# A gated cross-attention and mixture-of-experts block on one Trainium2 core: who places the value strips, and when three small pieces of routing work run

## The chip, the core and the metric

One core of a Trainium2 chip, one launch. Its engines run side by side, each in the order of its own instruction queue, and meet only through semaphores: TensorE (PE), VectorE (DVE), ScalarE (ACT), GpSimd (POOL) and SyncE (SP, which here only issues DMAs). The metric is the device time of one launch in microseconds (us). The kernel before takes 487.54 us, the median of 3 runs (487.33 to 488.08).

## The reference

Two residual steps on x of shape (8, 256, 256), all in float32:

```
q = layernorm(x) @ wq + bq;  k = ctx @ wk + bk;  v = ctx @ wv + bv        # 16 heads of 16, 77 context rows
score = q k^T / 4 * mask;  score = where(score == 0, -1e9, score)
x = x + tanh(g_xattn) * ((softmax(score) v) @ wo + bo)
n = layernorm(x);  probs = softmax(n @ router_w + router_b)               # 4 experts, the best 2 of each token
x = x + tanh(g_ffn) * sum over the 2 experts of gate * ((silu(n @ w1) * (n @ w3)) @ w2)
```

## The kernel before

**Two halves.** Attention runs batch by batch (b = 0 to 7); from about 158 us on the experts run over "slots" of 256 grouped tokens, 16 full ones and 3 short ones, with each float32 product split into three fp32r products. Everything is unrolled by hand: each engine's function is a list of calls whose order is the order of its queue.

**Attention of one batch.** `turn_x(b)` (PE, L1540) transposes the normalized x that ACT's `norm(b)` (L831) has written; ACT's `xT_copy(b)` takes it from the PSUM bank `ps_misc`; `project_q(b)` (PE, L1547) makes the queries in the same bank, and `q_copy(b)` (ACT, L849 and L850) takes them to `qT`. `scores(b, g)` (PE, L1561) makes the scores of eight heads (g = 0 or 1). For each of the four strips s of a batch, DVE's `mask_scores` (L1308), `sink_zeros` (L1314) and `find_lowest` (L1319) prepare the softmax, POOL's `lower(b, s)` (L1149) subtracts the minimum, PE's `turn_p` (L1573, L1581) transposes, ACT's `probT_exp` (L862, L867) takes the exponential into SBUF, and PE's `attend` (L1593) multiplies with the values. ACT's `weighed_copy` (L874) brings the result back, DVE's `invert_sums` (L1326) inverts the sums, `context(b, g)` (L307, on POOL; for the last batch on DVE) divides, `turn_ctx` (PE, L1607) and `project_o` (PE, L1615) follow, and DVE's `residual` (L1294) adds.

**The values.** `values(i)` (PE, L1715) projects the values of two batches into one of four PSUM banks (`ps_vals`, the fourth is `ps_misc`), ACT's `vals_copy` (L945) takes them to `vals`. `place_values` (L738) then copies them with DMAs into the block matrix `vblock`: 12 strips (`STRIPS`), each 1 to 77 rows of 544 bytes, for batches 0 to 3 (i = 0), and 12 more for 4 to 7 (i = 1). Before the change SP issues 8 strips of i = 0 and all of i = 1, and ACT issues the last 4 of i = 0. SP issues the loads of the expert weights and the fill of `grouped` behind them.

**Routing.** Batches go in pairs (group k). After a pair, DVE's `variance2`, POOL's `deviation2(k)` (L331, L333, L335), ACT's `norm2` (L347) and PE's `turn2` (L359) and `route_product` (L374) make the logits; DVE's `logit` (L384), `compare`, `order_of`, `choose` (L412, L414) and `lag` pick the experts; `rank` (PE) and `places` (POOL) find each token's row, and POOL's `scatter` (L514) sends the rows to `grouped` in DRAM by indirect DMA. DVE's `hand_out(i)`, `hand_out_begin`, `hand_out_owner` and `hand_out_rest` (L524 to L568) turn the counts into slots: 20 small instructions for i = 0, 1, 2 each, counted by the semaphore `handed`. SP's load of slot 0's tokens (L782) waits for the 20th.

**Where they stand.** Group 0's hand-out (i = 0) runs on DVE in b = 6 (`hand_out(0)` after strip 0, `hand_out_begin` and `hand_out_owner` after strip 1) and in b = 7 (`hand_out_rest` after strip 1). Group 1's routing (logit to lag) stands behind it in b = 6. In b = 7 POOL does gates, fill, `context(6, 0)`, `lower(7, 0)`, places, one scatter, `lower(7, 1)`, `deviation2(2)`, `context(6, 1)`, `lower(7, 2)`, `lower(7, 3)`, and then seven scatters; PE's `turn_ctx(6)` and, behind it, `attend(7, 1)` and `turn_p(7, 2)` wait in its queue for `context(6, 1)`.

Of the kernel before, what the change touches and what calls it, by code (L numbers as in the profile page):

```python
# [16 lines left out]
P = 128  # L17
# [21 lines left out]
BY_ACT = 4  # L39
# [61 lines left out]
def flamingo_block(nc, x, ctx_t, mask, rows, columns, wq, wk, wv, wo, rw, w1, w3, w2, small_in, tokens_in, pad_in, out, grouped):  # L101

    with ExitStack() as keep:
# [136 lines left out]
        ps_vals = [ps_probT, ps_route, ps_wide, ps_misc]  # L240
# [25 lines left out]
        kblock_done = sem("kblock_done")  # L266
        ld_vblock = [sem(f"ld_vblock{i}") for i in range(2)]
# [69 lines left out]
        def norm2(act, k, some):  # L337
            act.wait_ge(off2_done, k + 1)
            if k == 0:

                for landed in ld_vblock:
                    act.wait_ge(landed, 16 * len(STRIPS))
# [109 lines left out]
        def fill(pool, k):  # L452

            pool.wait_ge(rt_step, ROUTE * k + 16)
            if k == 0:

                for landed in ld_vblock:
                    pool.wait_ge(landed, 16 * len(STRIPS))
# [61 lines left out]
        def hand_out(dve, i):  # L520

            at = HAND * i
            dve.wait_ge(ranked, i + 1)
            dve.scalar_tensor_tensor(out=count[:], in0=base, scalar=1.0 - TILE, in1=first_row,  # L524
                                     op0=ALU.add, op1=ALU.subtract).then_inc(handed, 1)
            dve.wait_ge(handed, at + 1)
# [204 lines left out]
        def place_values(eng, i, some):  # L731
# [5 lines left out]
            for c, h, r0, r1 in some:  # L737
                eng.dma_start(vblock[r0 - c * P:r1 - c * P, c, h - HEAD0[c], mine], vals[r0 - h * SK:r1 - h * SK, h, mine]).then_inc(ld_vblock[i], 16)  # L738

        with nc.Block(no_gpsimd_drain=True) as block:  # L740
            @block.sync
            def _(sp):
# [22 lines left out]
                place_values(sp, 0, STRIPS[:-BY_ACT])  # L765
                place_values(sp, 1, STRIPS)
# [47 lines left out]
            def _(act):  # L814
# [32 lines left out]
                def q_copy(b):  # L847
                    act.wait_ge(q_done, b + 1)
                    act.activation(qT[:, 0, :], ps_misc[:, 0:SQ], ACT.Identity, bias=bqs[:, 0:1]).then_inc(q_copied, 1)  # L849
# [30 lines left out]
                def body(b, first=False, last=False):  # L880
# [3 lines left out]
                    if not last:  # L884
                        norm(b + 1)
# [3 lines left out]
                    if not last:  # L889
                        xT_copy(b + 1)  # L890
# [64 lines left out]
                q_copy(0)  # L955
                vals_copy(2)
                vals_copy(3)
                place_values(act, 0, STRIPS[-BY_ACT:])
# [159 lines left out]
            def _(pool):  # L1118
# [33 lines left out]
                def body(b, first=False, last=False):  # L1152
# [15 lines left out]
                    if b in BEGIN:  # L1168
# [3 lines left out]
                    if not first:  # L1172
                        context(pool, b - 1, 1)
                    lower(b, 2)
# [32 lines left out]
                keys(0, 1)  # L1207

# [59 lines left out]
            def _(dve):  # L1268
# [59 lines left out]
                def body(b):  # L1328
                    for s in range(NS):
# [22 lines left out]
                        if (b, s) == (B - 2, 0):  # L1352
                            hand_out(dve, 0)
                        if (b, s) == (B - 2, 1):
                            hand_out_begin(dve, 0)
                            hand_out_owner(dve, 0)
                        if (b, s) == (B - 1, 1):
# [31 lines left out]
                context(dve, B - 1, 0)  # L1389
                hand_out(dve, 1)  # L1390
# [510 lines left out]
```

## Time and profile before

| | |
|---|---|
| median of 3 runs | 487.54 us |
| the profiled execution's own time | 488.64 us |
| its span in the profile | 486.70 us |
| mean granted TensorE clock, share of full | 0.989 |
| busy PE, DVE, ACT, POOL | 460.7, 378.6, 307.0, 196.0 us |

The span is 1.94 us shorter than the time of the same execution; the rest lies around it. Times in the rows below count from the start of the span. A matmul that is queued counts as busy, so PE's 95% does not say that its array was full.

### The profile page before, as it was taken

What the parts mean: (1) busy time and instruction counts of PE and PEld (TensorE: products, weight loads), DVE (VectorE), ACT (ScalarE), POOL (GpSimd) and SP (SyncE); (2) the same over time, 40 slices, a digit from 0 to 9 for tenths busy, and PEclk for the clock granted to TensorE, in tenths of its full rate; (3) what the DMA queues carried; (4) which work ended last, traced back from release to release, by engine and by line L of the source; (5) the groups of instructions that cost most, each with busy time, mean ns of one, the idle gap of its engine ahead of it and who ended that gap; (6) DMA issues with size and microseconds to landing.
All of it is one profiled execution on the core that took longest, in us unless ns stands there. A gap on an engine that the chain in (4) does not pass through costs nothing.

```text
span 486.7 us, 11552 instructions
## 1 busy us (share of the span) xinstructions
PE 460.7 (95%) x3720; PEld 433.4 (89%) x3720; DVE 378.6 (78%) x876; ACT 307.0 (63%) x768; POOL 196.0 (40%) x204
## 2 busy tenths in 40 slices
PE   7899899989869999999999999999999999999995
PEld 5578797877767999899999999999999999999894
DVE  1577998978964888886888888888878878878772
ACT  2426555464435667686767767777767767776782
POOL 4428686597784045342146253113303303302312
PEclk9989999999979999999999999999999999999999
DMA  8619998842113104032023132122112102102112
GB/s 256 162 42 392 380 410 312 335 179 90 39 50 112 47 22 90 12 80 24 23 31 70 38 66 45 24 44 26 33 33 44 21 22 33 22 13 34 23 13 23
DMA packets 33968, 45.22 MB, mean 93 GB/s; under 512 B 10183, under 2 KB 30613, under 8 KB 33685
## 3 DMA queue, kind: packets, MB, share of 16 engines
q1 hardware_dynamic: 25999, 35.21, 21.6%
q0 software_dynamic: 6576, 8.92, 10.9%
q10 hardware_dynamic: 1344, 0.48, 0.5%
q8 instruction: 26, 0.43, 0.4%
q14 instruction: 23, 0.19, 0.1%
HBM read 32.91 MB, written 21.82 MB: 112 GB/s over the span
## 4 chain that ended last, share of the span: by engine, by line
PE 68%; DVE 16%; ACT 5%; issue 4%; POOL 3%; ACTq 1%; DMA 1%; DVEq 0%; SPq 0%; POOLq 0%
PE ps_rows L1764 22%; PE ps_wide L1784 7%; PE ps_probT L1764 7%; PE ps_misc L1784 7%; PE ps_wide L1593 5%; DVE w_lo L1404 3%; PE ps_misc L1615 2%; PE ps_misc L1547 2%; PE ps_rows L1813 2%; DVE w_lo L1400 2%; PE ps_probT L1573 2%; PE ps_wide L1824 1%; PE ps_rows L1561 1%; DVE score L1314 1%; DVE ps_rows L1409 1%
## 5 line engine op out<-in xcount | busy, mean ns | idle before, releaser
L1227 POOL DMA_INDIRECT out_x<-y_out,meta x35 | 64.0, 1830 | 190.9 <-ACT y_out L1026 185.8
L1404 DVE TENSOR_TENSOR w_lo<-w,w_hi 128x512 fp32r<-128x512 f32 x152 | 104.1, 685 | 13.4 <-issue 6.6
L1764 PE MATMUL ps_rows<-xt_hi,w_hi 128*128 128x256 f32 x384 | 110.6, 288 | 0.2 <-DVE xt_lo L1418 0.2
L1764 PE MATMUL ps_rows<-xt_hi,w_lo 128*128 128x256 f32 x384 | 108.6, 283 | 0.0
L1764 PE MATMUL ps_rows<-xt_lo,w_hi 128*128 128x256 f32 x384 | 108.6, 283 | 0.0
L975 ACT CAST w_hi<-w 128x512 fp32r x152 | 95.2, 627 | 4.2 <-issue 3.9
L1764 PEld LDWEIGHTS ps_rows<-xt_hi,w_hi 128*128 128x128 f32 x384 | 73.6, 192 | 0.4 <-DVE xt_lo L1418 0.4
L1764 PEld LDWEIGHTS ps_rows<-xt_lo,w_hi 128*128 128x128 f32 x384 | 73.6, 192 | 0.0
L1764 PEld LDWEIGHTS ps_rows<-xt_hi,w_lo 128*128 128x128 f32 x384 | 73.5, 192 | 0.0
L989 ACT ACTIVATE act_g<-ps_rows 128x256 f32<-128x256 f32 x96 | 37.3, 389 | 28.7 <-PE ps_rows L1764 24.0
L1004 ACT CAST hid_hi<-ps_rows 128x256 fp32r<-128x256 f32 x96 | 36.1, 376 | 27.1 <-DVE ps_rows L1409 26.3
L1413 DVE TENSOR_TENSOR hid_lo<-ps_rows,hid_hi 128x256 fp32r<-128x256 f32 x96 | 40.5, 422 | 15.6 <-ACT hid_hi L1004 15.6
L1149 POOL TENSOR_TENSOR score<-score,lowest 128x616 f32<-128x616 f32 x32 | 41.5, 1297 | 22.1 <-DVE lowest L1319 21.8
L1593 PEld LDWEIGHTS ps_wide<-vblock,probT 128*128 128x128 f32 (+1 forms) x320 | 39.7, 196 | 10.5 <-ACT probT L867 10.2
L1400 DVE TENSOR_TENSOR w_lo<-w2s,w_hi 128x512 fp32r<-128x512 f32 x64 | 44.0, 688 | 5.8 <-ACT w_hi L982 5.8
L1593 PE MATMUL ps_wide<-vblock,probT 128*128 128x102 f32 (+2 forms) x320 | 42.0, 278 | 6.0 <-ACT probT L867 5.9
L1409 DVE TENSOR_TENSOR ps_rows<-act_g,ps_rows 128x256 f32<-128x256 f32 x96 | 40.6, 423 | 7.3 <-ACT act_g L989 6.0
L982 ACT CAST w_hi<-w2s 128x512 fp32r x64 | 39.7, 620 | 0.0
L514 POOL DMA_INDIRECT grouped<-shared,place_at x32 | 33.9, 1061 | 9.8 <-issue 8.7
L1784 PE MATMUL ps_misc<-w_hi,hid_hi 128*128 128x256 f32 x128 | 37.0, 289 | 0.6 <-DVE hid_lo L1413 0.5
L1784 PE MATMUL ps_wide<-w_hi,hid_hi 128*128 128x256 f32 x128 | 36.6, 286 | 0.1
L1764 PE MATMUL ps_probT<-xt_hi,w_hi 128*128 128x256 f32 x128 | 36.2, 283 | 0.0
(241 smaller groups left out, 1160.9 us busy)
## 6 DMA issues: line engine op xcount, KB each, us to landing
grouped<-in_pad SPq DMA_DIRECT2D x1, 10296.0 KB
w<-in_L_ffn_w SPq DMA_DIRECT2D x8, 1024.0 KB, 12.2
w2s<-in_L_ffn_w SPq DMA_DIRECT2D x4, 1024.0 KB, 13.7
xg<-grouped SPq DMA_DIRECT2D x16, 256.0 KB, 2.7
out_x<-xall SPq DMA_DIRECT2D x8, 256.0 KB, 7.0
xall<-in_x SPq DMA_DIRECT2D x1, 1024.0 KB, 12.6
xall<-in_x SPq DMA_DIRECT2D x1, 768.0 KB, 7.9
ctxT<-in_ctx_t SPq DMA_DIRECT2D x2, 308.0 KB, 5.4
```

What stands on the lines that cost most here:

```text
L975: act.copy(w_hi[:, f % NB], unit_weights(e, f)).then_inc(w_hi_done, 1)
L982: act.copy(w2_hi[:, q % 2], pair_w2(e, q)).then_inc(w2_hi_done, 1)
L989: act.activation(act_g[:, f % 2, 0:n], ps_gu[f % NB][:, 0, 0:n], ACT.Silu).then_inc(silu_done, 1)
L1149: pool.tensor_tensor(score[:, s], score[:, s], lowest[:, s].unsqueeze(2).to_broadcast([P, HG, SK]), ALU.subtract).then_inc(lowered, 1)
L1227: pool.indirect_dma_start(out, bass.IndirectOffsetOnAxis(ap=meta[:, s % 2, t, E:E + 1].bitcast(U32), axis=0), y_out[:, s % 2, t, :], None, ...
L1400: dve.tensor_tensor(w2_lo[:, q % 2], pair_w2(e, q), w2_hi[:, q % 2].bitcast(F32), ALU.subtract).then_inc(w2_lo_done, 1)
L1404: dve.tensor_tensor(w_lo[:, f % NB], unit_weights(e, f), w_hi[:, f % NB].bitcast(F32), ALU.subtract).then_inc(w_lo_done, 1)
L1409: dve.tensor_tensor(ps_gu[f % NB][:, 1, 0:n], act_g[:, f % 2, 0:n], ps_gu[f % NB][:, 1, 0:n], ALU.mult).then_inc(hid_done, 1)
L1413: dve.tensor_tensor(hid_lo[:, f % NB, 0:n], ps_gu[f % NB][:, 1, 0:n], hid_hi[:, f % NB, 0:n].bitcast(F32), ALU.subtract).then_inc(hid_lo_d ...
L1593: mm = pe.matmul(ps_av[:, :, HEAD0[c]:HEAD0[c] + HEADS[c], :], probT[0:ROWS[c], s % 2, c, :], vblock[0:ROWS[c], c, 0:HEADS[c], b].rearrang ...
L1764: mm = pe.matmul(ps_gu[f % NB][:, m, 0:n], lhs, rhs[:, a, c, 0:n], start=(k == 0), stop=(k % (3 * DC) == 3 * DC - 1), skip_group_check=True)
L1784: mm = pe.matmul(ps_y[a][:, t], lhs, w, start=(f == 0 and t == 0 and i == 0), stop=(f == FC - 1 and i == 2), skip_group_check=True)
```

## The change

It does five things.

1. The last 4 strips of i = 0 are issued by POOL in place of ACT, after `keys(0, 1)` and before its first `lower`. They count on a semaphore of their own, `ld_vblock_end`, which `attend(0, 0)`, `norm2` and `fill` wait for as well.
2. ACT does `norm(1)` right after `q_copy(0)`, and `xT_copy(1)` after the copies of `values(1)`. PE does `turn_x(1)` ahead of `values(2)` and `project_q(1)` ahead of `values(3)`.
3. `values(3)` goes to the bank `ps_probT` (after the copies of `values(0)`), so `turn_x(1)` no longer waits for all value copies. `q_copy(b)` waits, for b above 0, for the scores of the batch before.
4. In b = 7, POOL does `context(6, 1)` before `deviation2(2)`.
5. The first instruction of a hand-out is a function of its own, `hand_out_count`. For i = 0 it alone stays in b = 6; the other four instructions of `hand_out(0)` go to b = 7 after strip 1, and begin, owner and rest to b = 7 after strip 3.

```diff
-        ps_vals = [ps_probT, ps_route, ps_wide, ps_misc]
+        ps_vals = [ps_probT, ps_route, ps_wide, ps_probT]
...
-        def hand_out(dve, i):
-
-            at = HAND * i
+        def hand_out_count(dve, i):
             dve.wait_ge(ranked, i + 1)
             dve.scalar_tensor_tensor(out=count[:], in0=base, ...).then_inc(handed, 1)
+
+        def hand_out(dve, i):
+            at = HAND * i
             dve.wait_ge(handed, at + 1)
...
-                place_values(sp, 0, STRIPS[:-BY_ACT])
-                place_values(sp, 1, STRIPS)
+                place_values(sp, 0, STRIPS[:-BY_POOL], ld_vblock[0])
+                place_values(sp, 1, STRIPS, ld_vblock[1])
...
                 def q_copy(b):
                     act.wait_ge(q_done, b + 1)
+                    if b:
+                        act.wait_ge(scores_done, RG * DC * b)
...
                 vals_copy(0)
                 vals_copy(1)
                 q_copy(0)
+                norm(1)
                 vals_copy(2)
                 vals_copy(3)
-                place_values(act, 0, STRIPS[-BY_ACT:])
+                xT_copy(1)
                 for b in range(B // 2, B):
                     vals_copy(b)
...
-                    if b in BEGIN:
+                    if b in BEGIN and not last:
                         deviation2(pool, BEGIN[b])
...
                     if not first:
                         context(pool, b - 1, 1)
+                    if last:
+                        deviation2(pool, BEGIN[b])
                     lower(b, 2)
...
                 keys(0, 1)
+                place_values(pool, 0, STRIPS[-BY_POOL:], ld_vblock_end)
                 body(0, first=True)
...
                         if (b, s) == (B - 2, 0):
-                            hand_out(dve, 0)
-                        if (b, s) == (B - 2, 1):
+                            hand_out_count(dve, 0)
+                        if (b, s) == (B - 1, 1):
+                            hand_out(dve, 0)
+                        if (b, s) == (B - 1, 3):
                             hand_out_begin(dve, 0)
                             hand_out_owner(dve, 0)
-                        if (b, s) == (B - 1, 1):
                             hand_out_rest(dve, 0)
...
                 scores(0, 0, True)
+                turn_x(1)
                 values(2)
-                pe.wait_ge(q_copied, 2)
+                project_q(1)
+                pe.wait_ge(vals_copied, 2)
                 values(3)
-                turn_x(1)
                 scores(0, 1, True)
-                project_q(1)
                 body(0, first=True)
```

## Rows read from the trace of the kernel before

**Rows 1.** Page, part 4: engines on the chain that ended last.

```profile
PE 68%; DVE 16%; ACT 5%; issue 4%; POOL 3%; ACTq 1%; DMA 1%; DVEq 0%; SPq 0%; POOLq 0%
```

**Rows 2.** Timeline, 14 to 34 us: start, us, engine, line, work, count, idle before.

```profile
14.13 1.89 PE L1547 MATMUL ps_misc<-xnT,wqs 128*128 128x256 f32 x8
16.43 0.47 ACT L850 ACTIVATE qT<-ps_misc,column_in 128x256 f32<-128x256 f32 x1
17.68 0.81 PE L1561 MATMUL ps_rows<-kblock,qT 32*128 32x154 f32 x16
18.54 3.79 ACTq L738 DMA_DIRECT2D vblock<-shared  x4
26.57 2.91 PE L1547 MATMUL ps_misc<-xnT,wqs 128*128 128x256 f32 x8
26.79 1.51 DVE L1308 TENSOR_TENSOR score<-ps_rows,maskt 128x616 f32<-128x616 f32 x2 [3.51 <-PE ps_rows L1561]
29.32 0.60 PE L1573 MATMUL ps_probT<-small,score 128*128 128x128 f32 x4
30.77 1.33 PE L1593 MATMUL ps_wide<-vblock,probT 128*128 128x68 f32 x10 [0.75 <-ACT probT L867]
33.53 1.51 DVE L1308 TENSOR_TENSOR score<-ps_rows,maskt 128x616 f32<-128x616 f32 x2 [0.27 <-PE ps_rows L1561]
```

**Rows 3.** Windows: stretch, length, busy PE, PEld, DVE, ACT, POOL, PEclk, DMA, GB/s.

```profile
22.00:25.00 3.00, 0.51 (x5) 0.42 (x4) 1.25 (x2) 2.17 (x6) 3.00 (x3) 1.00 0.19 49
107.00:108.40 1.40, 0.90 (x7) 0.47 (x5) 0.84 (x2) 0.99 (x4) 1.22 (x1) 1.00 0.00 0
126.00:128.00 2.00, 0.54 (x5) 0.39 (x3) 1.93 (x6) 0.27 (x1) 1.92 (x3) 1.00 0.19 68
138.00:141.00 3.00, 0.77 (x5) 0.52 (x5) 2.97 (x5) 0.77 (x2) 2.83 (x5) 1.00 0.34 87
141.00:148.00 7.00, 6.52 (x26) 6.04 (x27) 2.50 (x13) 2.61 (x6) 5.99 (x6) 0.51 0.11 39
```

**Rows 4.** Groups by line, POOL's DMAs: busy us, mean ns, idle before.

```profile
L1227 POOL DMA_INDIRECT out_x<-y_out,meta x35 | 64.0, 1830 | 190.9 <-ACT y_out L1026 185.8 <-issue 5.1
L514 POOL DMA_INDIRECT grouped<-shared,place_at x32 | 33.9, 1061 | 9.8 <-issue 8.7 <-POOL place_at L504 1.1
```

**Rows 5.** Timeline of b = 6, 113 to 128 us.

```profile
113.56 0.19 DVE L527 TENSOR_TENSOR begun<-count,small 128x32 f32<-128x32 f32 x1
115.88 0.16 DVE L538 TENSOR_REDUCE last_slot<-fresh_until 128x4 f32<-128x16 f32 x1
117.36 1.94 PE L374 MATMUL ps_route<-rws,ctxT 128*128 128x64 f32 x16
118.12 1.50 DVE L1308 TENSOR_TENSOR score<-ps_rows,maskt 128x616 f32<-128x616 f32 x2
121.07 0.16 DVE L384 TENSOR_TENSOR logits<-ps_route,row_in 128x16 f32<-128x16 f32 x1
127.70 0.39 PE L475 MATMUL ps_route<-places_base,one_row 1*128 1x20 f32 x2 [1.46 <-DVE chosen_b L414]
```

**Rows 6.** Timeline: deviation2(0) in b = 3, then b = 7, 137 to 146 us.

```profile
69.95 1.02 POOL L331 TENSOR_TENSOR rstd<-vareps,half 128x4 f32<-128x4 f32 x1
137.08 1.22 POOL L1149 TENSOR_TENSOR score<-score,lowest 128x616 f32<-128x616 f32 x1
138.26 1.62 POOL L331 TENSOR_TENSOR rstd<-vareps,half 128x4 f32<-128x4 f32 x1
138.90 0.24 DVE L1326 RECIPROCAL rden<-weighed 128x16 f32<-128x16 f32 x1
140.81 0.61 POOL L307 TENSOR_TENSOR ctxn<-weighed,rden 128x256 f32<-128x256 f32 x1
141.48 1.11 PE L1607 MATMUL ps_misc<-small,ctxn 128*128 128x128 f32 x4 [2.35 <-POOL ctxn L307]
144.42 1.06 PE L1573 MATMUL ps_probT<-small,score 128*128 128x128 f32 x4
```

More of the change, by code:

```diff
@@ L38 @@
 STRIPS = [(c, h, max(c * P, h * SK), min(c * P + ROWS[c], (h + 1) * SK)) for c in range(NC) for h in range(HEAD0[c], HEAD0[c] + HEADS[c])]
-BY_ACT = 4
+BY_POOL = 4
 NS = 2 * QT
@@ L266, in flamingo_block @@
         kblock_done = sem("kblock_done")
+        ld_vblock_end = sem("ld_vblock_end")
         ld_vblock = [sem(f"ld_vblock{i}") for i in range(2)]
@@ L339, in norm2 @@
             if k == 0:
-                for landed in ld_vblock:
-                    act.wait_ge(landed, 16 * len(STRIPS))
+                act.wait_ge(ld_vblock_end, 16 * BY_POOL)
+                act.wait_ge(ld_vblock[0], 16 * (len(STRIPS) - BY_POOL))
+                act.wait_ge(ld_vblock[1], 16 * len(STRIPS))
             if k > 1:
@@ L455, in fill @@
             if k == 0:
-                for landed in ld_vblock:
-                    pool.wait_ge(landed, 16 * len(STRIPS))
+                pool.wait_ge(ld_vblock_end, 16 * BY_POOL)
+                pool.wait_ge(ld_vblock[0], 16 * (len(STRIPS) - BY_POOL))
+                pool.wait_ge(ld_vblock[1], 16 * len(STRIPS))
             if k > 1:
@@ L729, in is_slot, with place_values @@
             return isinstance(s, int) and s == n
-        def place_values(eng, i, some):
+        def place_values(eng, i, some, landing):
             eng.wait_ge(vblock_cleared, 1)
@@ L737, in place_values @@
             for c, h, r0, r1 in some:
-                eng.dma_start(vblock[r0 - c * P:r1 - c * P, c, h - HEAD0[c], mine], vals[r0 - h * SK:r1 - h * SK, h, mine]).then_inc(ld_vblock[i], 16)
+                eng.dma_start(vblock[r0 - c * P:r1 - c * P, c, h - HEAD0[c], mine], vals[r0 - h * SK:r1 - h * SK, h, mine]).then_inc(landing, 16)
         with nc.Block(no_gpsimd_drain=True) as block:
@@ L883, in body @@
                         turned2_copy(act, BEGIN[b - 1], 2)
-                    if not last:
+                    if not last and not first:
                         norm(b + 1)
@@ L888, in body @@
                         probT_exp(b - 1, 3, False)
-                    if not last:
+                    if not last and not first:
                         xT_copy(b + 1)
@@ L1389, in _ @@
                 context(dve, B - 1, 0)
+                hand_out_count(dve, 1)
                 hand_out(dve, 1)
@@ L1485, in routing @@
                     if u == 8:
+                        hand_out_count(dve, 2)
                         hand_out(dve, 2)
@@ L1530, in turn_x @@
                         pe.wait_ge(q_copied, 2 * b)
-                    if b == 1:
-                        pe.wait_ge(vals_copied, B)
                     if b == 2:
@@ L1588, in attend @@
                         pe.wait_ge(weighed_done, n)
-                    if s == 0 and b % (B // 2) == 0:
-                        pe.wait_ge(ld_vblock[b // (B // 2)], 16 * len(STRIPS))
+                    if s == 0 and b == 0:
+                        pe.wait_ge(ld_vblock_end, 16 * BY_POOL)
+                        pe.wait_ge(ld_vblock[0], 16 * (len(STRIPS) - BY_POOL))
+                    if s == 0 and b == B // 2:
+                        pe.wait_ge(ld_vblock[1], 16 * len(STRIPS))
                     for c in range(NC):
```

## The prediction

> **What bounds the kernel now.** I read the page's chain shares first: PE carries 68% of the chain that ended last, DVE 16%, POOL 3%, ACT's DMA issue 1% [rows 1]. The expert half is PE on end and the change leaves it alone, so I followed the chain and the timeline only to 158 us, and looked at the three places that the diff touches. There the reader should see three stalls.
>
> First, in the prelude ACT issues four strips for 3.79 us from 18.54 on, and the copies of the later values, norm(1) and with it turn_x(1) stand behind them. PE is busy for 0.51 of the 3 us from 22 to 25 [rows 2, 3], its granted clock then falls to half, and project_q(1) takes 2.91 us where project_q(0) took 1.89. DVE has idled 3.51 us when mask_scores for strips 2 and 3 of batch 0 begins at 26.79 [rows 2]. From there to 33.53, the masks of batch 1, it has only 0.27 us idle [rows 2]: DVE is the bound of that stretch, PE's attend(0, 0) at 30.77 is not.
>
> Second, in b = 6 DVE is on the chain from 112.7 to 130, and the hand-out stands in its queue: four instructions from 113.56, nine from 115.88 to 118.12, before the masks of strips 2 and 3 [rows 5].
>
> Third, in b = 7 POOL is on the chain: lower(7, 1) at 137.08, deviation2(2) from 138.26, context(6, 1) only at 140.81, and PE, idle 2.35 us, starts turn_ctx(6) at 141.48 [rows 6]. The clock then is 0.51 over the 7 us from 141 to 148 [rows 3].
>
> **Prelude, edits 1 to 3.** q_copy(0) ends at 16.90 [rows 2]. norm(1) is 2 activations of some 0.55 us, so 18.05, in time for the copies of values(1), which are late by 0.2 us at most. scores(0, 0) starts at 17.68 and lasts 0.81 [rows 2]. Behind it PE runs without a wait: turn_x(1) at 18.5 (0.45 us of pipeline), values(2) 1.74 (eight matmuls as in project_q(0), whose 1.89 includes the last one's drain), project_q(1) 1.74, values(3) 1.74, so scores(0, 1) starts at 24.15 and the masks about 1 us behind it, at 25.15. That is 1.6 us before 26.79. The DVE block of 6.74 us to the masks of batch 1 [rows 2] keeps its length less the 0.27 of idle time: 31.65 for 33.53, a gain of 1.9. Behind it DVE had another 0.6 us of waiting for PE, which may go too, but POOL's bias additions come earlier and would then lie beside sink_zeros of batch 1; I leave it out and keep it as the lower end (gain 2.5). Batches 1 to 5 have no absolute time in them, so this moves along.
>
> POOL's four issues have no row. The nearest are its indirect DMAs, 1.06 us each plus 0.27 idle, 1.33 in all; the dearest are those of the experts at 1.83 [rows 4]. ACT's own issues of the same strips, 3.79 / 4 = 0.95 us, are the cheap end [rows 2]. Queued behind them are lower(0, 0), keys(1, 0) and lower(0, 1), for which PE's turn_p waits. With 1.33 each from 18.9, lower(0, 0) (1.22 [rows 6]) runs at 24.2 to 25.4 and attend(0, 0) follows 1.45 us after the transposes begin, as 29.32 to 30.77 [rows 2], so at 27. With 0.95 it is limited by PE instead, at 26.7. With 1.83, lower ends at 27.4 and attend is at 29. Before it was 30.77, and DVE's gain of 1.9 needs about 28.9. So the price hardly matters inside the rows' ends: 1.9 at the likely price, 1.7 at the dear end. SP's eighth strip is issued by 18.8 + 8 x 0.95 = 26.4 at ACT's pace, and some 2 us of flight would still be inside 28.9. SP begins its twelve other strips when the last values are copied (25.1), 0.2 to 0.6 later than now, and the weights and the fill of grouped move by that. Nobody waits: all DMA traffic is over by 107, 1.4 us before the first scatter at 108.4 [rows 3], and the fill stands ahead of the out writes in that traffic. The new wait of q_copy is for matmuls that PE has done before the transposes that q_copy's predecessor used, so nothing.
>
> One rule speaks against POOL. The Trainium skill, "SBUF — State Buffer", section "Who interferes with whom", says that GpSimd cannot write DMA descriptors while VectorE runs a two-port operation, and names copy, cast and tensor_scalar on SBUF. DVE runs none of these between 18.9 and 24, only the masks from PSUM, sink_zeros and find_lowest (no run shows a plain DMA of POOL beside them), so by the rule as written the sum stays; if each of these five operations blocked POOL too, some 4.7 us (estimate) would be added and the gain of the prelude would be about nil.
>
> **b = 6, edit 5.** Removed from DVE before the masks of strips 2 and 3: four instructions (113.56 to about 114.4, 0.86 us) and nine (115.88 to 118.12, 2.24), 3.1 us [rows 5]. Not all of it is gained, since logit(1) waits for route_product(1) on PE, 117.36 + 1.94 = 119.3. So logit comes at 119.35 and not 121.07: 1.7 us [rows 5]. rank waits 1.46 us for chosen_b and starts at 127.70 [rows 5]; chosen_b comes 1.7 earlier and PE reaches rank at 127.70 - 1.46 = 126.2, so 1.5 to 1.6 us. I take 1.6, as POOL's gates follow DVE and not PE. Ends: 1.0, if POOL's scatters and bias_add, which do not move by as much, hold lower(6, 3); 2.2, if compare's two instructions, which lie beside POOL work now, get shorter. The four instructions come back in b = 7 after strip 1, where 0.73 us of hand_out_rest goes: 0.13 us on DVE. The other fifteen take some 2.4 us (2.24 for the nine of rows 5 with one that was held up, 0.73 for the six of rest, less the hold-up) and run after strip 3, where DVE has nothing else until PE's attend(7, 1) is back. SP then loads slot 0's tokens around 142 in the new time, for a transpose that PE reaches 5 to 6 us later.
>
> **b = 7, edit 4.** With everything 1.6 earlier, lower(7, 1) ends at 136.7. context(6, 1) needs the sums of invert_sums(6, 1), at 138.90 + 0.24 now [rows 6] and at 137.3 to 137.6 then. It is done at 138.0 and turn_ctx(6) starts at 138.05 where it was 141.48. The next that is late is turn_p(7, 2) on PE, for lower(7, 2), which stands behind deviation2(2). That took 138.26 to 140.81, 2.55 us, with rstd 1.62; in b = 3, with DVE out of the way, rstd was 1.02 [rows 6] and the whole 1.6. In its new place rstd lies beside sink_zeros and the rest beside find_lowest: 2.2. So lower(7, 2) runs 140.2 to 141.4, and turn_p(7, 2) starts at 141.45 for 144.42: 3.0 us, of which 1.4 is edit 4's (ends 1.0 and 1.9 with 2.55 and 1.6).
>
> **The clock.** PE would now idle from the end of attend(7, 1), 139.7, to 141.45: 1.75 us. Its idle of 2.35 us here, and of 3 - 0.51 = 2.5 us in the prelude, was followed by the lower of its two levels (1.2 GHz); the 1.46 us before rank left it at the higher one (2.4 GHz) [rows 3, 5, 6]. 1.75 is nearer to that. If the clock holds, the work from turn_p(7, 2) to the end of project_o(6), 4.2 us now at half clock [rows 3, 6], takes 2.5: 1.6 us more. Norm2's copies and slot 0 hang on that chain.
>
> **Sum.** 1.9 + 1.6 + 1.4 + 1.6 = 6.5 us. I take 0.2 off for the small shifts left out (SP, the 0.13 us on DVE): 6.3. On the profiled execution that is 486.70 - 6.3 = 480.4 of span and 488.64 - 6.3 = 482.3 of time. The median of the runs lies 1.1 below that execution: 487.54 - 6.3 = 481.2.
>
> **Rivals.**
> - *The clock falls all the same in b = 7.* For it: 1.75 us is no row, and PE's idle time before it adds 0.6 us near 137.4. Against it: both falls had longer gaps. Then 1.6 is lost: 487.54 - 4.7 = 482.8.
> - *The prelude gives nothing*, because POOL's issues or the landing of its strips hold attend(0, 0) to 30 or later (the price per issue above 2.1 us), while b = 6 and 7 go as above: 487.54 - 4.4 = 483.1; with the clock's fall, 484.7.
> - *Slower: POOL's issues become the bound of the prelude.* Each costs p, and attend(0, 0) comes at 18.9 + 4p + 1.22 + 1.45. It passes 30.77 from p = 2.3, and the loss eats 3.0 us of b = 6 and 7 (clock fallen) from p = 3.05. At p = 3.6, 2.2 us are lost: 489.7. For it: nothing shows a plain DMA on this queue. Against it: 67 indirect ones at 1.06 and 1.83 [rows 4].
> - *Nothing moves*: the first two stalls turn out to be cover for another wait up to 158 us, as DVE's POOL partners in b = 1 and b = 6: 487.5.
>
> **How the numbers follow.** The forecast 0.46, the clock's fall 0.32, a prelude without gain 0.13, slower 0.05, nothing 0.04. The predicted time is the first's, 481.2. The low end takes the cheap ends together (2.5 + 2.0 + 1.7 + 1.6 = 7.8, less a bit): 479.9. The high end takes in the clock's fall and most of the third case: 484.6. A change of less than 0.2% (1.0 us) cannot be told from none. Faster 0.91, same 0.04, slower 0.05.
>
> **What would show it.** Masks of batch 0, strips 2 and 3, at 25.2 and of batch 1 at 31.7; the granted clock 1.00 from 25 to 28; POOL's four issues 1.0 to 1.4 us each and attend(0, 0) near 27. In b = 6, logit(1) right behind route_product(1), and rank straight behind attend(6, 1). In b = 7, turn_ctx(6) 0.6 us behind invert_sums(6, 1), PE idle under 2 us before turn_p(7, 2), and project_o(6) 1.9 us long. The first matmul of slot 0, now near 158.1, at 151.8. I am wrong if attend(0, 0) waits for a strip, if the clock reads 0.5 in b = 7, or if the gain at 54 us is gone again at 112.

## The result, and the profile after

The changed kernel takes 483.47 us, the median of 5 runs (482.7 to 485.29), against 487.54 us (487.1 to 488.08) for the kernel before in the same comparison: a ratio of 0.9925, with an interval of 0.9901 to 0.9949. The profiled execution took 483.3 us, its span 481.4 us, at a mean granted clock of 0.992. The forecast was 481.2 us, in a range of 479.9 to 484.6: the time lies in the range, 2.3 us above the forecast, and the signs that the first rival named (the clock falls all the same in b = 7, 482.8 us) are what the profile shows.

The start of q_copy(0) varies by up to 0.9 us between the executions profiled here (15.39 to 16.33), so places are also compared by their distance from it; it stands at 16.06 in the trace before and at 15.72 after.

| place | before | after | change behind q_copy(0) |
|---|---|---|---|
| masks of batch 1 | 33.53 | 31.19 | -2.00 |
| last mean_off of the prelude | 47.75 | 44.70 | -2.71 |
| rank of group 1 | 127.70 | 123.69 | -3.67 |
| turn_p(7, 2) | 144.42 | 139.22 | -4.86 |
| first matmul of slot 0 | 158.15 | 152.92 | -4.89 |

So by these two traces 2.71 us come up to the last mean_off (the prelude's place), 0.96 from there to rank (b = 6), 1.19 from b = 7 up to turn_p(7, 2), and 0.03 from there to slot 0, where 1.6 was forecast. They are differences between one execution of each kernel; how much of them a fall of the clock makes up is taken up with x4 and x7. The 0.34 us by which this execution started earlier belongs to no edit. The chain that ended last is made up much as before. Its engines, page of the changed kernel, part 4, the answer to [rows 1]: PE keeps its 68%, DVE has two points more and POOL one less.

```profile
PE 68%; DVE 18%; ACT 5%; issue 4%; POOL 2%; DMA 1%; ACTq 1%; DVEq 0%; SPq 0%; POOLq 0%
```

**Prelude.** Timeline of the changed kernel, 18 to 32 us (start, us, engine, line, work, count, idle before), the answer to [rows 2]:

```profile
18.80 2.41 POOL L743 DMA_DIRECT2D vblock<-shared  x4 [1.64 <-ACT shared L952]
...
20.30 1.89 PE L1559 MATMUL ps_misc<-xnT,wqs 128*128 128x256 f32 x8
...
24.80 1.51 DVE L1319 TENSOR_TENSOR score<-ps_rows,maskt 128x616 f32<-128x616 f32 x2 [1.85 <-PE ps_rows L1573]
...
26.16 1.33 PE L1608 MATMUL ps_wide<-vblock,probT 128*128 128x68 f32 x10 [0.75 <-ACT probT L874]
...
31.19 1.50 DVE L1319 TENSOR_TENSOR score<-ps_rows,maskt 128x616 f32<-128x616 f32 x2
```

The four issues take 0.60 us each on POOL, project_q(1) has its full clock (1.89 us for 2.91), and the masks wait 1.85 us for 3.51. attend(0, 0), forecast near 27, comes at 26.16, 4.6 us earlier than before, and what ends its wait is ACT's exponential, not a strip.

**b = 6.** Timeline of the changed kernel, 114 to 124 us, the answer to [rows 5]:

```profile
114.32 1.94 PE L376 MATMUL ps_route<-rws,ctxT 128*128 128x64 f32 x16
...
116.30 0.17 DVE L386 TENSOR_TENSOR logits<-ps_route,row_in 128x16 f32<-128x16 f32 x1 [0.57 <-PE ps_route L376]
...
116.51 3.17 DVE L394 TENSOR_TENSOR equal<-logits 128x64 f32<-128x64 f32 x1
...
116.58 0.63 POOL L308 TENSOR_TENSOR ctxn<-weighed,rden 128x256 f32<-128x256 f32 x1
...
117.15 1.22 POOL L1157 TENSOR_TENSOR score<-score,lowest 128x616 f32<-128x616 f32 x1
...
118.33 1.26 POOL L1151 TENSOR_TENSOR xall<-xall,row_in 128x512 f32<-128x512 f32 x1
...
119.61 0.21 DVE L395 TENSOR_TENSOR above<-logits 128x64 f32<-128x64 f32 x1
```

The logits come right behind the product, as forecast: 1.72 us earlier than before behind the last mean_off. Then `equal`, 64 elements, takes 3.17 us, where `above`, of the same shape, takes 0.21 right behind it. It ends at 119.68, 0.09 us after POOL's third operation in a row has ended. In the trace before the two took 2.56 us together, now 3.38: this step eats 0.8 of the 1.7 us.

**b = 7.** Timeline of the changed kernel, 134 to 153 us, the answer to [rows 6], and its windows around the clock's fall (columns as in [rows 3]), the answer to [rows 3]:

```profile
134.37 0.66 PE L1585 MATMUL ps_probT<-small,score 128*128 128x128 f32 x4 [0.70 <-POOL score L1157]
...
134.90 0.24 DVE L1337 RECIPROCAL rden<-weighed 128x16 f32<-128x16 f32 x1
...
135.22 0.62 POOL L308 TENSOR_TENSOR ctxn<-weighed,rden 128x256 f32<-128x256 f32 x1 [0.91 <-DVE rden L1337]
...
135.80 1.62 POOL L332 TENSOR_TENSOR rstd<-vareps,half 128x4 f32<-128x4 f32 x1
...
135.90 1.12 PE L1622 MATMUL ps_misc<-small,ctxn 128*128 128x128 f32 x4 [0.76 <-POOL ctxn L308]
...
139.22 1.12 PE L1585 MATMUL ps_probT<-small,score 128*128 128x128 f32 x4 [0.17 <-POOL score L1157]
...
140.34 3.02 PE L1630 MATMUL ps_misc<-wos,ctxnT 128*128 128x256 f32 x8
```

```profile
133.50:136.00 2.50, 1.03 (x8) 0.64 (x8) 2.50 (x5) 1.04 (x3) 1.59 (x3) 0.96 0.15 54
136.00:143.00 7.00, 6.83 (x27) 6.13 (x28) 6.52 (x25) 2.69 (x6) 6.21 (x7) 0.53 0.05 19
```

The order did what was wanted: turn_ctx(6) starts 0.76 us behind the end of invert_sums(6, 1), after a wait of 0.76 us where it was 2.35, and turn_p(7, 2) waits 0.17 us. But the clock goes to its lower level (1.2 GHz) at 135.8 and stays there until 142.6. That is before the wait that the prediction had weighed, and behind waits of 0.70 and 0.76 us; in the stretch from 133.5 to 136 PE was busy for 1.03 of 2.5 us. project_o(6) then takes 3.02 us.

### The profile page after: what moved, and what is told of

The parts are those of the page before. It is cut to its first block, busy times and chain, and to the rows that moved or that the text cites. A ratio compares the mean times of both kernels' runs of the same rounds, so it can differ in the third digit from the quotient of the medians.

```text
span 481.4 us, 11562 instructions
## 1 busy us (share of the span) xinstructions
PE 459.7 (95%) x3720; PEld 433.0 (90%) x3720; DVE 379.9 (79%) x876; ACT 306.8 (64%) x768; POOL 198.8 (41%) x208
## 4 chain that ended last, share of the span: by engine, by line
PE 68%; DVE 18%; ACT 5%; issue 4%; POOL 2%; DMA 1%; ACTq 1%; DVEq 0%; SPq 0%; POOLq 0%
PE ps_rows L1779 22%; PE ps_wide L1799 7%; PE ps_probT L1779 7%; PE ps_misc L1799 7%; PE ps_wide L1608 4%; DVE w_lo L1417 3%; PE ps_misc L1630 2%; PE ps_rows L1828 2%; DVE score L1325 2%; PE ps_misc L1559 2%; DVE w_lo L1413 2%; PE ps_probT L1585 2%; PE ps_wide L1839 1%; DVE score L1319 1%; PE ps_rows L1573 1%
```

## The experiments

The first four ran on one chip (kernel before there: 487.01 us), x5 to x8 on one (487.47), x9 to x11 on one (486.87), x12 alone (487.70). The theory going in: three separate gains, one for each place, and the clock's fall in b = 7 as a loss of its own that the order on POOL doesn't cure. The rival: one edit carries all.

**x1_changed**: the changed kernel again, beside its parts. No edit.

> The changed kernel itself, on the chip on which its parts run. Theory: 4.1 us less than before (the ratio measured so far, 0.9925), spread over some 2.5 us from run to run, because TensorE's granted clock falls for one stretch more in some executions than in others. Rival, that the spread is noise of other origin: then runs with the same mean granted clock differ as much as runs with different ones.

483.06 us, ratio 0.9911 (0.9883 to 0.9939). In its profile TensorE stays at the lower clock for 10.2 us in b = 7 and not for 6.8, and slot 0 comes 0.9 us later behind q_copy(0) (138.09 for 137.20): between these two executions a longer fall goes with about a microsecond.

**x2_prelude_only**: edits 1 to 3 alone.

```diff
-                    if b in BEGIN and not last:
+                    if b in BEGIN:
                         deviation2(pool, BEGIN[b])
...                  (context and hand-out as in the kernel before)
```

> Edits 1 to 3 alone (strips by GpSimd, the prelude's order, the bank), b = 6 and b = 7 as before. Theory, from the two traces: the prelude is worth 2.7 to 3.0 us, more than the 1.9 of the prediction, so 484.6 beside 487.5, and the first product of slot 0 at 155.1 to 155.4 where it was 158.15. Rival, the prediction's own sum: 1.9 us, 485.6. Second rival, the parts depend on each other and the prelude alone loses part of its gain again in b = 6: under 1.5 us.

485.22 us, ratio 0.9956 (0.9938 to 0.9974): -1.8 us. The last mean_off stands 28.98 behind the start of q_copy(0), as in the changed kernel.

**x3_context_first**: edit 4 alone, on the kernel before.

```diff
-                    if b in BEGIN:
+                    if b in BEGIN and not last:
                         deviation2(pool, BEGIN[b])
...
                         context(pool, b - 1, 1)
+                    if last:
+                        deviation2(pool, BEGIN[b])
```

> Edit 4 alone: in b = 7 GpSimd divides context(6, 1) before deviation2(2). Theory: turn_ctx(6) 1.6 us earlier (139.9 for 141.48), and turn_p(7, 2) 1.2 us earlier, for lower(7, 2) stands behind deviation2 in either order; 486.3 beside 487.5, with the clock falling as before. Rival, that the clock holds now that the wait is short: 1.6 us more, 484.7.

487.39 us, ratio 1.0002 (0.9972 to 1.0032): no gain in the time. Its profile has the step itself; timeline of this kernel, b = 7:

```profile
140.00 0.66 PE L1609 MATMUL ps_misc<-small,ctxn 128*128 128x128 f32 x4 [0.77 <-POOL ctxn L307]
...
143.33 1.11 PE L1575 MATMUL ps_probT<-small,score 128*128 128x128 f32 x4 [0.92 <-POOL score L1149]
...
144.45 3.49 PE L1617 MATMUL ps_misc<-wos,ctxnT 128*128 128x256 f32 x8
```

turn_p(7, 2) is 1.21 us earlier behind the last mean_off (95.46 for 96.67), the forecast's 1.4 nearly. But project_o(6) takes 3.49 us, nearly all of it at the lower clock (the fall lasts from 140.8 to 147.6), where it took 3.10, and slot 0 keeps 0.77 of the gain. That is within the interval of the time.

The 12 executions of this kernel lie between 483.62 us, at a mean granted clock of 0.999, and 490.25, at 0.982, and those of like clock agree within a microsecond (484.69 and 484.96 at 0.995, 489.06 and 489.14 at 0.985). This speaks for the theory put under x1, that the spread from run to run goes with the clock; the order on POOL does not keep the clock up.

**x4_handout_spread**: edit 5 alone.

```diff
                         if (b, s) == (B - 2, 0):
+                            hand_out_count(dve, 0)
+                        if (b, s) == (B - 1, 1):
                             hand_out(dve, 0)
-                        if (b, s) == (B - 2, 1):
+                        if (b, s) == (B - 1, 3):
                             hand_out_begin(dve, 0)
                             hand_out_owner(dve, 0)
-                        if (b, s) == (B - 1, 1):
                             hand_out_rest(dve, 0)
```

> Edit 5 alone: the hand-out of group 0 leaves b = 6. Theory, from the changed trace: 3.1 us of VectorE work goes but logit(1) gains 1.7 us only, and equal (the first of compare), which then meets GpSimd's context, lower and bias_add back to back, lasts some 3.2 us instead of 1.26, so that rank and all behind it gain 1.0 us: 486.5 beside 487.5. Rival, the prediction: 1.6 us, 485.9, with equal as long as before.

485.78 us, ratio 0.9969 (0.9949 to 0.9990): -1.2 us. Rank stands 78.96 behind the last mean_off, for 79.95 before: a gain of 0.99. Timeline of this kernel, b = 6: here `equal` is quick, and `above`, the next, waits in its place.

```profile
118.11 0.23 DVE L392 TENSOR_TENSOR equal<-logits 128x64 f32<-128x64 f32 x1
...
118.22 0.63 POOL L307 TENSOR_TENSOR ctxn<-weighed,rden 128x256 f32<-128x256 f32 x1
118.25 3.08 DVE L393 TENSOR_TENSOR above<-logits 128x64 f32<-128x64 f32 x1
```

Its prelude is the old one, and in this execution the clock did not fall at 25 us, as it did in the trace before: project_q(1) takes 1.99 us for 2.91 in [rows 2]. It fell later, at 37.2, for 3.4 us. Timeline of this kernel, and the window of that fall:

```profile
25.59 1.99 PE L1552 MATMUL ps_misc<-xnT,wqs 128*128 128x256 f32 x8
...
32.18 1.49 DVE L1310 TENSOR_TENSOR score<-ps_rows,maskt 128x616 f32<-128x616 f32 x2
...
39.60 1.50 DVE L1310 TENSOR_TENSOR score<-ps_rows,maskt 128x616 f32<-128x616 f32 x2 [0.65 <-PE ps_rows L1566]
```

```profile
37.20:40.60 3.40, 3.40 (x28) 2.74 (x26) 2.71 (x4) 1.08 (x4) 3.40 (x5) 0.51 1.03 422
```

So the comparison is clean only up to the masks of batch 1. They stand 16.45 us behind the start of q_copy(0) here, 17.47 in the trace before and 15.47 in the changed kernel: of the 2.00 us gained at that place, 0.98 is there with the clock up in both, and 1.02 goes with the fall at 25 us, which the profiled execution of the kernel before had and this one lacks. The last mean_off is 30.59 behind q_copy(0), 1.10 less than before and 1.61 more than in the changed kernel, but x4's own fall, with 0.65 us of waiting in it, lies ahead of that place.

The falls may well go with the old prelude's waits (PE waits 2.49 us for norm(1) in the trace before and here). All four traces that keep the old prelude have a fall ahead of the last mean_off, at 25.0, 24.8 (x3), 23.8 (x11) and 37.2 us (x4), and none of the eight with the new one has. Then the 1.02 us are the change's as well, but their size and place differ from one execution to the next, and no run separates the two.

From the last mean_off to slot 0 this kernel takes 108.15 us, the changed one 108.22 and the one before 110.40. Without edit 4, turn_p(7, 2) comes 16.72 us behind rank, with it 15.53, but the fall here (136.2 to 143.0) is over when project_o(6) starts, which takes 1.89 us. PE was busy for 4.91 of the 6.8 us of this fall, and for 6.53 of the 6.8 of the changed kernel's. What edit 4 gains at turn_p(7, 2) is thus not seen at slot 0 in this pair of traces.

**x7_pool_issue_only** and **x8_order_only** take the prelude apart: edit 1 alone, and edits 2 and 3 with ACT still issuing, after the second copy of values.

```diff
-                place_values(act, 0, STRIPS[-BY_ACT:])
...
                 keys(0, 1)
+                place_values(pool, 0, STRIPS[-BY_ACT:], ld_vblock_end)
```

```diff
                 vals_copy(3)
+                place_values(act, 0, STRIPS[-BY_POOL:], ld_vblock_end)
                 xT_copy(1)
...
-                place_values(pool, 0, STRIPS[-BY_POOL:], ld_vblock_end)
```

> The kernel before with edit 1 alone: GpSimd issues the four strips, order and banks of the prelude as before. Measured from the start of q_copy(0) to the last mean_off, which is 31.69 us before and 28.97 in the changed kernel, of which 1.1 us is a fall of the clock in the prelude that some executions have and others not. Theory: ScalarE is free of 3.8 us, but the copies of values(3) must still wait for that product, so norm(1) and turn_x(1) come only 0.5 us earlier: 31.1 with the fall, 30.0 without. Rival: the issues by ScalarE were the whole stall, and this alone brings the 2.7 us: 29.0.

> The changed kernel with the four strips issued by ScalarE again, at their old place, right after the copies of values(1): edits 2 and 3 without edit 1. Theory: xT_copy(1) now stands behind 3.8 us of issuing, project_q(1) waits for it and values(3) and scores(0, 1) behind that, so the masks of strips 2 and 3 come no earlier than before: 31.4 to 32 us from q_copy(0) to the last mean_off (31.69 before, 28.97 changed). Rival: the order alone brings most of it, since turn_x(1) is no longer behind the copies: 29.5.

x7 took 484.99 us and x8 486.27, one run each. Timelines of the two kernels, x7 first:

```profile
19.08 2.40 POOL L741 DMA_DIRECT2D vblock<-shared  x4 [1.61 <-ACT shared L948]
...
25.30 1.50 DVE L1311 TENSOR_TENSOR score<-ps_rows,maskt 128x616 f32<-128x616 f32 x2 [2.07 <-PE ps_rows L1564]
```

```profile
18.78 3.80 ACTq L743 DMA_DIRECT2D vblock<-shared  x4
...
22.62 0.59 ACT L850 COPY xnT<-ps_misc 128x512 f32<-128x512 f32 x1 [3.95 <-issue]
...
23.26 1.99 PE L1559 MATMUL ps_misc<-xnT,wqs 128*128 128x256 f32 x8 [2.23 <-ACT xnT L850]
...
27.86 1.50 DVE L1319 TENSOR_TENSOR score<-ps_rows,maskt 128x616 f32<-128x616 f32 x2 [4.34 <-PE ps_rows L1573]
```

Neither has a fall of the clock up to the last mean_off. The masks of batch 1 (31.69 in x7, 34.25 in x8) stand 15.68 behind the start of q_copy(0) in x7 and 17.95 in x8, against 16.45 in x4 and 15.47 in the changed kernel. At that place edit 1 alone gives 0.77 us; the new order alone costs 1.50, since project_q(1) then stands in PE's queue ahead of values(3) and scores(0, 1) and waits for a copy behind ACT's issues; together they give 0.98. The issue moved is what pays, and the new order adds 0.21 once ACT is free. These are places in one execution each; the two times, one run each, are too few for a verdict.

**x9_pool_issues_eight** asks how near the rival "POOL's issues become the bound" was.

```diff
-BY_POOL = 4
+BY_POOL = 8
```

> The changed kernel with BY_POOL = 8: GpSimd issues eight of the first set's strips, SyncE four. Theory: an issue on GpSimd costs 0.60 us here and nothing waits for GpSimd in the prelude until lower(0,0), so eight issues end 2.4 us later than four (at 23.6) and the path hardly feels it: lower(0,0) starts at 23.7 to 24.3 instead of near 22.5, the masks of batch 0's strips 2 and 3 stay at 24.8 (9.1 behind the start of q_copy(0)), the last mean_off stays 29.0 behind q_copy(0), within 0.3. Rival (the price that the slower rival of the prediction gave an issue, 3.05 us): lower(0,0) beyond 30 and mean_off 3 us or more later. Middle case: the issues stay cheap but turn_p(0,0) is then the last to wait, attend(0,0) comes up to 1.2 us later and mean_off with it by 0.5 to 1.2.

483.3 us, one run. Timeline of this kernel:

```profile
18.80 4.44 POOL L743 DMA_DIRECT2D vblock<-shared  x8 [1.61 <-ACT shared L952]
23.25 1.24 POOL L1157 TENSOR_TENSOR score<-score,lowest 128x616 f32<-128x616 f32 x1
...
24.80 1.51 DVE L1319 TENSOR_TENSOR score<-ps_rows,maskt 128x616 f32<-128x616 f32 x2 [1.85 <-PE ps_rows L1573]
...
26.16 1.33 PE L1608 MATMUL ps_wide<-vblock,probT 128*128 128x68 f32 x10 [0.74 <-ACT probT L874]
```

Twice the issues (0.56 us each) move nothing: the masks and attend(0, 0) are where they were. lower(0, 0) starts 1.75 us later than with four (21.50), and the last mean_off stays 28.96 behind q_copy(0), for 28.98.

**x5_pe_filled** gives TensorE work in place of its waits in b = 7: products of a zero tile whose result nobody reads.

```diff
+                def keep_busy(n):
+                    pe.wait_ge(masked, NS * B)
+                    for i in range(n):
+                        pe.matmul(ps_scores[0][:, 1], blank[:, 0:P], blank[:], start=True, stop=True)
...
+                    if last:
+                        keep_busy(4)
                     if not first:
                         turn_ctx(b - 1, last)
...
+                    if last:
+                        keep_busy(8)
                     turn_p(b, 2, first)
```

> The changed kernel with twelve products of a blank tile more on TensorE in b = 7 (four ahead of turn_ctx(6), eight ahead of turn_p(7, 2)), into a bank that nobody reads. Theory: the granted clock falls there because TensorE is idle for short stretches, not because of one long one; filled, it stays at 1.00 from 130 to 150, turn_p(7, 2) to the end of project_o(6) takes 2.5 us instead of 4.1, and the kernel gains 1.6 us on the changed one, 481.5 beside 483.1 (487.0 before). Cost of the fill: nothing while it ends before the waits do, up to 0.5 us if not. Rival: the clock falls all the same (something other than idle time lowers it), and the time is that of the changed kernel or 0.5 us above it.

482.16 us (481.51 to 483.05), ratio 0.9892 (0.9869 to 0.9915). Windows of this kernel, and its timeline:

```profile
133.50:136.00 2.50, 1.79 (x13) 1.56 (x13) 2.50 (x4) 0.83 (x3) 1.59 (x2) 1.00 0.15 54
136.00:143.00 7.00, 7.00 (x47) 6.06 (x46) 6.57 (x24) 3.24 (x10) 6.35 (x8) 1.00 0.05 19
```

```profile
137.81 2.11 PE L1616 MATMUL ps_rows<-blank 128*128 128x512 f32 x8
...
139.76 0.60 PE L1585 MATMUL ps_probT<-small,score 128*128 128x128 f32 x4
...
140.31 1.89 PE L1635 MATMUL ps_misc<-wos,ctxnT 128*128 128x256 f32 x8
```

The clock holds, project_o(6) takes 1.89 us, and slot 0 starts 135.67 behind q_copy(0), 1.53 us before the changed kernel: the size of the term that failed. This is one execution; x10, below, has the same products and did not keep the clock.

**x12_filled_four_six**: the same with six products, not eight, in the second place.

> The changed kernel with four blank products ahead of turn_ctx(6) as in x5_pe_filled and six, not eight, ahead of turn_p(7,2). Theory: in x5 the eight ran from 137.81 to 139.92 and turn_p(7,2) started at 139.76, 0.2 us later against q_copy(0) than in the changed kernel (123.67 against 123.50); six end 0.5 us sooner and cost nothing, and the clock still holds in batch 7. Then turn_p(7,2) starts at 123.5 behind q_copy(0), project_o(6) takes 1.9 us, the clock is 1.00 from 130 to 144, and the time is 481.9 to 482.5, 0.6 to 1.2 us under the changed kernel's 483.06 to 483.47. Rival: the part of the clock's falls that the blank products do away with is given back by them, as x11_before_filled showed no gain in the kernel before; then 483.0 to 483.6, and the falls that are left stand at other places.

482.50 us (481.88 to 484.71), ratio 0.9905 (0.9877 to 0.9932). turn_p(7, 2) stands at 123.52 behind q_copy(0), the clock is 1.00 from 136 to 143, and slot 0 is at 135.58. Its worst execution, 484.71, had a mean clock of 0.991, so falls still come; where that one fell was not traced. In the profiled one the clock is low only from 477.5 us on, in the last 2.5 us of the span.

**x11_before_filled**: the blank products of x5 in the kernel before, which keeps its order.

> The kernel before with the same blank products on TensorE in batch 7 (four ahead of turn_ctx(6), eight ahead of turn_p(7,2)) and nothing else. Theory: the clock's fall in batch 7 is the same loss in both kernels and is cured by work on TensorE, not by the order on GpSimd; then the clock stays at 1.00 from 135 to 150, project_o(6) takes 1.9 us instead of its 3.6, and the time is 1.3 to 1.8 us under before (ratio 0.996 to 0.997). Rival: in the kernel before, TensorE also stands for 2.35 us ahead of turn_ctx(6), 1.2 of it left after the blank products, and the clock falls all the same; then the time is within 0.4 us of before, and the context ahead of the deviation is needed for the cure to hold.

487.19 us, ratio 0.9999 (0.9979 to 1.0019). Windows of this kernel and, for its b = 7, the timeline:

```profile
24.00:30.80 6.80, 6.67 (x32) 5.21 (x33) 4.03 (x8) 0.66 (x2) 0.95 (x2) 0.51 0.13 34
129.80:133.20 3.40, 3.40 (x10) 2.58 (x9) 2.89 (x7) 0.60 (x1) 1.64 (x6) 0.52 0.03 5
141.00:148.00 7.00, 6.55 (x38) 5.49 (x39) 5.20 (x18) 3.10 (x8) 5.52 (x5) 1.00 0.21 57
```

```profile
144.16 2.10 PE L1601 MATMUL ps_rows<-blank 128*128 128x512 f32 x8
...
146.10 0.60 PE L1573 MATMUL ps_probT<-small,score 128*128 128x128 f32 x4
```

In the profiled execution the clock holds in b = 7, and from the last mean_off to slot 0 it takes 109.31 us for 110.40 before, 1.1 less. The time does not show it: over the 12 executions the mean clock rises from 0.988 to 0.992 and the median stays. The theory's forecast of the clock held and its forecast of the time failed. In the same execution the clock fell at 23.8 and at 129.6; the first fall is longer than in the trace of before (the last mean_off stands 33.18 behind q_copy(0), for 31.69). Whether such falls took the gain back in the other executions, or the products themselves cost it in this kernel, where they end only just as turn_p(7, 2) starts, is open.

**x6_bias_late** takes one of POOL's three operations away from behind `equal`: bias_add(7) goes behind keys(7, 1).

```diff
-                    elif not last and not first:
+                    elif not last and not first and b != B - 2:
                         bias_add(b + 1)
...
                         keys(b + 1, 1)
+                    if b == B - 2:
+                        bias_add(b + 1)
```

> The changed kernel with bias_add(7) of b = 6 moved behind keys(7, 1), so that GpSimd reads SBUF for two operations in a row (context, lower) when compare begins, not three. Theory of the port: VectorE's operation with two SBUF inputs waits until GpSimd's queue has a gap, so equal (or above) lasts 1.9 us instead of 3.1 to 3.2 and rank comes 0.5 to 1.1 us earlier, until TensorE's attend(6, 1) bounds it; 482.4 beside 483.1. Rival: the wait has nothing to do with what GpSimd runs (a semaphore or a slow operand form): the length stays at 3.1 us and nothing moves.

483.41 us, ratio 0.9920 (0.9890 to 0.9949). Timeline of this kernel:

```profile
116.19 1.95 DVE L394 TENSOR_TENSOR equal<-logits 128x64 f32<-128x64 f32 x1
...
122.47 1.26 POOL L1151 TENSOR_TENSOR xall<-xall,row_in 128x512 f32<-128x512 f32 x1
122.57 1.18 DVE L426 TENSOR_TENSOR own_logit<-each 128x8 f32<-128x8 f32 x1
```

`equal` gets shorter by 1.22 us, nearly the length of the operation that was moved (1.26), and now `own_logit` takes 1.18 us beside it, where it took 0.17. So the rival, that the length has nothing to do with what POOL runs, is out. Rank gains 0.6 us, the gates, which need own_logit, 0.2, and the time nothing that can be told.

**x10_filled_chosen_direct** tried to get round the same wait with an operation of one input, on top of x5.

```diff
-            dve.tensor_tensor(chosen_b[:], pick[:, :, 0], pick[:, :, 1], ALU.add).then_inc(rt_step, 1)
+            dve.tensor_scalar(chosen_b[:], order[:], float(TOP) - 0.5, 1.0, ALU.is_lt, ALU.mult).then_inc(rt_step, 1)
```

> The changed kernel, with the blank products of x5_pe_filled on TensorE in batch 7, and chosen_b made straight from the order by one VectorE operation with one input (order < 1.5) where it was the sum of two picks. Theory (a VectorE operation with two inputs in SBUF waits for GpSimd's lower, 1.14 us instead of 0.2; one with a single input doesn't wait): chosen_b takes 0.2 us at batch 6, rank(1) starts 0.9 us earlier against q_copy(0) than with the fill alone (107.98 there), and the operation behind it (each, two inputs) takes up the wait instead, at 1.1 us. Of this 0 to 0.9 us reaches the slots, since the gates may have to wait for the sum of each. With the fill's 1.3: 481.3 to 482.2 us. Rival (chosen_b took 1.1 us for its own output type, bf16, or for what stood ahead of it on VectorE): chosen_b still takes 1.1 us, rank does not move, time as x5 (482.2).

482.44 us, ratio 0.9908 (0.9881 to 0.9934). Timeline of this kernel, and the window in which its clock falls:

```profile
122.31 1.21 POOL L1157 TENSOR_TENSOR score<-score,lowest 128x616 f32<-128x616 f32 x1
122.42 1.13 DVE L416 TENSOR_SCALAR chosen_b<-order 128x16 bf16<-128x16 f32 x1
...
134.81 1.91 PE L1616 MATMUL ps_rows<-blank 128*128 128x512 f32 x4
```

```profile
133.50:136.00 2.50, 1.79 (x9) 1.52 (x9) 2.50 (x4) 1.04 (x3) 1.59 (x3) 0.80 0.15 54
```

The theory that one input is enough fell: the tensor_scalar takes as long beside `lower` (1.13 us for 1.14). The rival as put (the bf16 output or the queue ahead) is not excluded for this operation by this run alone, though the two-input operations that write f32 wait in the same way. The Trainium skill, "SBUF — State Buffer", section "Who interferes with whom", names tensor_scalar among the operations that can take the port pair shared with GpSimd, when its operands meet certain conditions, beside those with two SBUF inputs, and says of tensor_reduce that on this chip it never does. The 1.13 us here agree with the first; no run here puts a tensor_reduce in this place.

Its profiled execution also shows that the fill is no sure cure. The clock falls at 135.0, within 0.2 us of the start of the first product and behind waits of 0.74 and 0.71 us, and stays low until 138.4. Yet up to that moment PE's work here and in x12 is the same, with starts that agree within 0.01 us in the two traces (134.29 and 134.30 for turn_p(7, 1), 134.81 and 134.82 for the products), and in x5 it is the same 0.46 us later; those two kept the clock. The four products take 1.91 us for 1.18, turn_p(7, 2) stands 125.19 behind q_copy(0) for 123.67 in x5, and slot 0 137.19, where the changed kernel has it (137.20).

**The best version.** x5, x10 and x12, the three with blank products, have medians of 482.16, 482.44 and 482.50 us, the changed kernel 483.06 and 483.47. Their intervals against the kernel before overlap, and they ran on other chips than x1, so a gain of 0.6 to 1.3 us over it is likely, not shown.

## Why the prediction came out as it did

- *Prelude* (forecast -1.9, ends 1.7 to 2.5; measured -2.71): at the masks of batch 1, where the term was worked out, the number was right, -2.00. By x4, 1.02 us of it goes with the fall of the clock at 25 us, which differs between executions, and 0.98 is there without it. Another 0.7 us came behind that place. DVE's wait of 0.58 us there, which the text had seen and left out, is gone; in the trace it ended with ACT's weighed_copy, not with PE. The sum was made against one execution with that fall in it. By the medians the prelude gives 1.8 us (x2).
- *Price of an issue on POOL*: 0.60 us, below the cheap end of 0.95. The bounds missed it, but the step that used them (inside the ends the price hardly matters) was right, and x9 shows how far. The slower rival, break-even at 3.05 us an issue, is out. That DVE's operations might each block the issues, which would have made the prelude's gain nil, did not come: the issues took 0.60 us each beside masks, sink_zeros and find_lowest.
- *b = 6* (forecast -1.6, ends 1.0 to 2.2; measured -0.96): logit moved as forecast, but compare's two operations took 3.38 us (3.17 + 0.21), while in the trace before they took 2.56 (1.26 + 1.30). The prediction had this wait on the list with the sign turned round: it hoped that they get shorter. Nothing in the diff touches them; being earlier put `equal` beside three operations of POOL in a row, where before `equal` and `above` had one each. x6, which moves one of the three away, takes 1.22 us off `equal`.
- *b = 7, edit 4* (forecast -1.4; measured -1.19): right at turn_p(7, 2), inside its ends; x3 gives 1.21 there for the edit alone. At slot 0 it is less sure: x3 keeps 0.77 of it and its time shows no gain, and x4, without the edit, reaches slot 0 as soon behind the last mean_off as the changed kernel. The prediction took the edit's gain and the clock's as terms that add up; in the traces the earlier order puts more of PE's work inside the fall.
- *Clock in b = 7* (forecast -1.6; measured 0): the step that failed. It argued from the length of one gap, 1.75 us between falls after 2.35 and none after 1.46. That gap was never put to the test: the clock fell earlier, at 135.8, behind waits of 0.70 and 0.76 us, and at the lower clock attend(7, 1) took 2.24 us for 1.23, which is why the gap ahead of turn_p(7, 2) shrank to 0.17. x5 kept the clock and got 1.53 us, the size of the term; x10, with the same work on PE up to the fall, lost it. So neither the length of one gap nor PE's work just ahead tells whether the clock falls; what does is open.
- *The sum*: 2.71 + 0.96 + 1.19 + 0.03 = 4.89 us, and 0.34 of an earlier start give the 5.2 at slot 0 and the 5.3 between the two profiled executions (488.64 and 483.3). The forecast was 6.3, from 6.5 before the 0.2 taken off. Against the 6.5 the misses are 0.8 too little for the prelude, and too much by 0.6 for b = 6, 0.2 for edit 4 and 1.6 for the clock; the first, mostly the 0.7 us that the text had left out, is of opposite sign and brought the sum nearer than its terms, and that was luck. The low end of the range adds 2.0 and 1.7 where the text gives ends of 2.2 and 1.9, which changes nothing here. Between the medians it is 4.07 (487.54 - 483.47): the profiled execution of the kernel before lay 1.1 above its median and had the prelude's fall, so the gain read from it is larger than the one between typical executions. The prediction moved its starting point from 488.64 to 487.54 for that, and left the gain as it was.
- *Rivals*: the prelude that gives nothing is out (x2); nothing moves is out. The one-edit rival of the experiments is out too, since x2 and x4 are each faster beyond their interval: x2, x3 and x4 give -1.8, +0.4 and -1.2 us by medians, -2.6 together against -3.95 for x1 on the same chip, a difference that their intervals (0.9 to 1.5 us either way) allow.

## What to carry to other kernels

When work on one engine moves, look at what it will now lie beside on the others: the small VectorE operations that follow a moved wait can take more than their own length beside GpSimd's (3.17 us for 0.2). A gain from the clock should be entered in a sum as a chance and not as a term, since traces of like kernels kept it and lost it, and the profiled execution may hold falls that other executions lack. An edit that moves work earlier can move it into such a fall. And a queue with a long issue in it (ACT's 3.79 us) should be emptied before the order around it is changed: alone, the order put the masks of batch 1 back by 1.50 us.

## What the runs showed of the hardware that I had not expected

- A VectorE operation of 0.2 us can take as long as several GpSimd operations in a row: 3.17 us beside context, lower and bias_add, 1.95 beside the first two (x6), 3.08 for `above` (x4). The Trainium skill, "SBUF — State Buffer", section "Who interferes with whom", says that a VectorE operation with two SBUF inputs contends with a GpSimd one that reads SBUF, and, of VectorE's two-port modes, that whichever issues first has the shared pair for its whole length while the other is blocked. If that held here too, `equal`, which starts at 116.51 by the trace, ahead of context at 116.58, would have gone first, or at the latest have ended behind context, at 117.2; the trace has it at 119.68. In the kernel before, `equal` (1.26 us) ended as `lower` ended, though bias_add stood next in POOL's queue. What decides this is open.
- GpSimd issues a plain DMA of a strip in 0.60 us, where ACT takes 0.95 for the same four and SP 0.79 each for its own (15.87 us for 20 in x2).
- TensorE's clock fell in b = 7 behind waits of at most 0.76 us. In the old prelude it fell at 25 us in one trace and only at 37 in another (x4), and with the same blank products ahead of turn_ctx(6) it held in two (x5, x12) and fell in a third (x10).
